# Scaled queries, a row minimum as the exponential's bias, and one broadcast product in the softmax of a decoder layer

## What is computed

```python
q = _mxfp4_matmul(x, wq_codes, wq_scales) + bq      # w = codes * scales repeated over 32 rows
k = _mxfp4_matmul(x, wk_codes, wk_scales) + bk
v = _mxfp4_matmul(x, wv_codes, wv_scales) + bv
scores = einsum('bqhd,bkhd->bhqk', q, k) / sqrt(128)
attn = softmax(scores, axis=-1)
out = einsum('bhqk,bkhd->bqhd', attn, v)
x = x + _mxfp4_matmul(out, wo_codes, wo_scales) + bo
```

## Time and profile before

| | us |
|---|---|
| median of 3 runs | 530.16 |
| lowest and highest run | 528.49, 530.91 |
| span of the profiled execution (first to last instruction) | 527.9 |
| busy PE / DVE / ACT / POOL | 489.7 / 405.2 / 283.8 / 191.0 |
| length of one attention group, second to seventh | 38.8 |

### The profile page before, as it was taken

The page is one execution under the profiler, slowest core; times in us unless marked ns, Lnnn a source line. Parts: engine busy times, 40 slices in busy tenths (PEclk is TensorE's granted clock), DMA queues, the critical chain, the costliest instruction groups (busy, mean ns, idle before and its releaser), DMA issues.

```text
span 527.9 us, 11484 instructions
## 1 busy us (share of the span) xinstructions
PE 489.7 (93%) x3222; PEld 431.4 (82%) x3222; DVE 405.2 (77%) x1040; ACT 283.8 (54%) x804; POOL 191.0 (36%) x232
## 2 busy tenths in 40 slices
PE   6899999999999999999999998979998999898985
PEld 6688899899898898898898898769875667776764
DVE  6689988988988988988988888787784753344465
ACT  2667656655655666666656564655425545522231
POOL 3417512312313313303303034426116666365640
PEclk9999999999999999999999999999989999999999
DMA  6441211210211211211100793299953456445544
GB/s 191 120 116 57 74 32 31 71 30 30 70 30 30 70 30 30 70 30 39 60 0 0 268 324 129 89 296 305 292 186 100 146 175 213 132 128 158 153 145 159
DMA packets 63269, 60.77 MB, mean 115 GB/s; under 512 B 5552, under 2 KB 60544, under 8 KB 63104
## 3 DMA queue, kind: packets, MB, share of 16 engines
q1 hardware_dynamic: 59024, 49.64, 31.0%
q0 software_dynamic: 3936, 10.55, 7.2%
q10 hardware_dynamic: 272, 0.13, 0.1%
HBM read 47.82 MB, written 20.87 MB: 130 GB/s over the span
## 4 chain that ended last, share of the span: by engine, by line
PE 63%; DVE 18%; issue 6%; ACT 6%; POOL 3%; DMA 1%; another core or an unknown queue 1%; DVEq 0%; SPq 0%; ACTq 0%; POOLq 0%
PE bank L998 12%; PE bank L1000 11%; PE bank L999 11%; PE bank L1239 11%; PE bank L1247 6%; DVE qk_lo L1759 4%; DVE rmax L1767 3%; DVE nmax L1771 3%; PE bank L1079 3%; ACT qk_hi L1497 2%; ACT prob L1505 2%; PE bank L1243 2%; DVE pT_lo L1792 1%; PE bank L1004 1%; PE bank L1373 1%
## 5 line engine op out<-in xcount | busy, mean ns | idle before, releaser
L1505 ACT ACTIVATE prob<-bank,nmax 128x256 f32<-128x256 f32 x128 | 59.5, 470 | 105.2 <-DVE nmax L1771 103.3
L711 POOL TENSOR_TENSOR w_lo<-st_c,w_hi 128x512 fp32r<-128x512 f32 x32 | 41.2, 1286 | 197.0 <-ACT w_hi L1468 197.0
L1239 PE MATMUL bank<-moe_w,xT 128*128 x252 | 66.0, 385 | 2.0 <-DVE xT L2067 1.8
L1759 DVE SCALAR_TENSOR_TENSOR qk_lo<-bank,b_col,qk_hi 128x512 fp32r<-128x512 f32 x64 | 47.8, 748 | 14.3 <-ACT qk_hi L1497 13.5
L998 PE MATMUL bank<-hT_hi,w_lo 128*128 128x512 f32 x128 | 52.7, 412 | 4.5 <-DVE qk_lo L1759 3.3
L1767 DVE TENSOR_REDUCE rmax<-bank 128x2 f32<-128x512 f32 x64 | 43.8, 685 | 13.8 <-PE bank L1000 13.3
L1239 PEld LDWEIGHTS bank<-moe_w,xT 128*128 128x128 f32 x252 | 45.2, 190 | 8.7 <-issue 2.9
L1000 PE MATMUL bank<-hT_hi,w_hi 128*128 128x512 f32 x128 | 50.6, 395 | 0.0
L999 PE MATMUL bank<-hT_lo,w_hi 128*128 128x512 f32 x128 | 50.5, 394 | 0.0
L1497 ACT ACTIVATE qk_hi<-bank,b_col 128x512 fp32r<-128x512 f32 x64 | 44.0, 687 | 8.6 <-PE bank L1000 7.2
L1785 DVE TENSOR_SCALAR prob<-prob,rinv 128x256 f32<-128x256 f32 x128 | 46.3, 403 | 2.3
(11 more groups left out here) (272 smaller groups left out, 1493.2 us busy)
## 6 DMA issues: line engine op xcount, KB each, us to landing
y_dram<-ysb SPq DMA_DIRECT2D x63, 128.0 KB
moe_w<-in_w_gate SPq DMA_DIRECT2D x8, 512.0 KB, 8.1
moe_w<-in_w_up SPq DMA_DIRECT2D x8, 512.0 KB, 7.8
moe_w<-in_w_down SPq DMA_DIRECT2D x4, 1024.0 KB, 9.0
st_c<-in_wq_codes SPq DMA_DIRECT2D x16, 128.0 KB
st_c<-in_wk_codes SPq DMA_DIRECT2D x16, 128.0 KB
st_c<-in_wv_codes SPq DMA_DIRECT2D x8, 256.0 KB
st_c<-in_wo_codes SPq DMA_DIRECT2D x8, 256.0 KB
```

Of the source, the lines that this page charges most:

```text
L1239: mm = pe.matmul(o, xT_of(kt), w, start=kt == 0, stop=kt == KT - 1)
L1505: ex = act.activation(prob[:, i % 4, qt, :], bS[i % 2][:, qt * S:(qt + 1) * S], ACT.Exp, bias=nmax[:, i % 2, qt:qt + 1], scale=SCALE, accu ...
L1759: dve.scalar_tensor_tensor(out=qk_lo[:, hp, m, n * HALF:(n + 1) * HALF], in0=src[:, :], scalar=b_col[:, bass.ds(g_h + m * H, 1)], in1=qk_h ...
```

## The change

The query weights' scales and the query bias are multiplied by minus the softmax scale, once for each chunk (POOL) and once for all (DVE). The scores in the bank are then the negated scaled ones, so their row minimum is the bias that the exponential needs, with -1 as its scale; `rmax`, `nmax`'s own instruction and the semaphore between them go. The normalisation of a pair becomes one product of 128x512 with the reciprocals broadcast over the keys. POOL's four numbers are loaded one by one.

```diff
@@ -288,7 +288,6 @@
         h_seg = pT_lo[:, :, :, :].rearrange("p a b k -> p a (b k)")
 
         yg = [nc.alloc_sbuf_tensor_at(f"yg{n}", [P, 2, NT, D], F32, offset=at) for n, at in enumerate(yg_at)]
-        rmax = sb("rmax", [P, 2, 2])
         nmax = sb("nmax", [P, 2, 2])
         rsum = sb("rsum", [P, 2, 2])
         rinv = sb("rinv", [P, 2, 2])
@@ -417,7 +416,7 @@
         a_copy, t_turn, t_tab = sem("a_copy"), sem("t_turn"), sem("t_tab")
         p_rows = sem("p_rows")
         p_many = sem("p_many")
-        p_wm = sem("p_wm")
+        p_wm, p_q = sem("p_wm"), sem("p_q")
         a_wh = sem("a_wh")
         p_wl = sem("p_wl")
         v_ln = sem("v_ln")
@@ -425,7 +424,7 @@
         t_ln, a_ln, v_lnlo = sem("t_ln"), sem("a_ln"), sem("v_lnlo")
         t_b, v_b = sem("t_b"), sem("v_b")
         t_sc = sem("t_sc")
-        v_m1, v_max = sem("v_m1"), sem("v_max")
+        v_max = sem("v_max")
         a_exp = sem("a_exp")
         v_ri, v_p = sem("v_ri"), sem("v_p")
         t_pT, a_pT, v_pT = sem("t_pT"), sem("a_pT"), sem("v_pT")
@@ -694,9 +693,19 @@
 
         @block.gpsimd
         def _(pool):
+            scaled = [0]
+
+            def scale_queries(c):
+
+                scaled[0] += 1
+                pool.tensor_scalar(st_s[c][:, 0, :], st_s[c][:, 0, :], -SCALE, None, ALU.mult).then_inc(p_q, 1)
+                pool.wait_ge(p_q, scaled[0])
+
             def prep(c, wm, load_count, into):
 
                 wait(pool, d_w[c], load_count)
+                if c in (H0, H1):
+                    scale_queries(c)
                 if c == WC:
                     codes_v, scale_v = st_c[c][:, :, :], st_s[c][:, :, :]
                 elif c == VC:
@@ -882,10 +891,9 @@
                 pool.indirect_dma_start(out=x_all[:, t, :], out_offset=None, in_=x2_dram,
                                         in_offset=bass.IndirectOffsetOnAxis(ap=dest[:, t:t + 1], axis=0)).then_inc(d_xt, 16)
 
-            at = [pool.alloc_register(f"need{k}") for k in range(TOPK)]
             pool.wait_ge(v_slot, S_NEED)
             apart(pool)
-            pool.reg_load(at, need[0:1, :])
+            needed = [pool.value_load(need[0:1, k:k + 1], min_val=1, max_val=TILES) for k in range(TOPK)]
             pool.wait_ge(d_xt, 16 * NT)
             own(pool.tensor_scalar(y_slot[:, :, :], ordered, -1.0, None, ALU.mult))
             for n, (t, k) in enumerate(gather_order):
@@ -894,7 +902,7 @@
                 if k == 3:
                     pool.wait_ge(v_sh, NT)
                 pool.wait_ge(t_gu, SH + min(USED, FIRST_BESIDE + n * 15 // 16))
-                pool.wait_ge(y_done, pool.snap(at[k], min_val=1, max_val=TILES))
+                pool.wait_ge(y_done, needed[k])
                 apart(pool)
                 pool.indirect_dma_start(out=home(k)[:, t, :], out_offset=None, in_=y_dram,
                                         in_offset=bass.IndirectOffsetOnAxis(ap=y_slot[:, t, k:k + 1], axis=0)).then_inc(d_yg[t][place_of(k)], 16)
@@ -1503,7 +1511,7 @@
                 wait(act, t_pT, p - 3 if not (pl.first and i < 4) else 0)
                 for qt in range(2):
                     ex = act.activation(prob[:, i % 4, qt, :], bS[i % 2][:, qt * S:(qt + 1) * S], ACT.Exp,
-                                        bias=nmax[:, i % 2, qt:qt + 1], scale=SCALE,
+                                        bias=nmax[:, i % 2, qt:qt + 1], scale=-1.0,
                                         accum_out=rsum[:, i % 2, qt:qt + 1])
                 ex.then_inc(a_exp, 1)
 
@@ -1729,7 +1737,8 @@
             statistics()
             variances()
             dve.wait_ge(t_b, 1)
-            dve.tensor_copy(b_col[:, :], bJ[0][:, 0:3 * H]).then_inc(v_b, 1)
+            dve.tensor_scalar(b_col[:, 0:H], bJ[0][:, 0:H], -SCALE, None, ALU.mult)
+            dve.tensor_copy(b_col[:, H:], bJ[0][:, H:3 * H]).then_inc(v_b, 1)
             ln_low(dve, 0, 0, FIRST[0])
             reciprocals()
             rows()
@@ -1764,11 +1773,8 @@
             def maxima(pl, i):
                 p = pl.pair(i)
                 wait(dve, t_sc, p + 1)
-                dve.tensor_reduce(rmax[:, i % 2, :], bS[i % 2][:, :].rearrange("p (q k) -> p q k", q=2),
-                                  AX.X, ALU.max).then_inc(v_m1, 1)
-                wait(dve, v_m1, p + 1)
-                wait(dve, a_exp, p - 1 if not (pl.first and i < 2) else 0)
-                dve.tensor_scalar(nmax[:, i % 2, :], rmax[:, i % 2, :], -SCALE, None, ALU.mult).then_inc(v_max, 1)
+                dve.tensor_reduce(nmax[:, i % 2, :], bS[i % 2][:, :].rearrange("p (q k) -> p q k", q=2),
+                                  AX.X, ALU.min).then_inc(v_max, 1)
 
             for pos, t in enumerate(PRO_TILES):
                 if pos == 2:
@@ -1781,10 +1787,8 @@
                 wait(dve, a_exp, pl.pair(j) + 1)
                 dve.reciprocal(rinv[:, j % 2, :], rsum[:, j % 2, :]).then_inc(v_ri, 1)
                 wait(dve, v_ri, pl.pair(j) + 1)
-                for qt in range(2):
-                    sc = dve.tensor_scalar(prob[:, j % 4, qt, :], prob[:, j % 4, qt, :],
-                                           rinv[:, j % 2, qt:qt + 1], None, ALU.mult)
-                sc.then_inc(v_p, 1)
+                dve.tensor_tensor(prob[:, j % 4, :, :], prob[:, j % 4, :, :],
+                                  rinv[:, j % 2, :].unsqueeze(2).to_broadcast([P, 2, S]), ALU.mult).then_inc(v_p, 1)
 
             def prob_low(pl, j):
```

## The result

The changed kernel took 516.8 us (median of 4 runs, 515.8 to 518.6) beside 529.4 us for the kernel before on the same chip (4 runs, 528.5 to 530.9): a ratio of 0.9745, with a 95% interval of 0.9711 to 0.9779. That is 12.5 us by the medians and 13.5 by the ratio (which is computed over the runs and isn't the quotient of these two medians, 0.976), where 10.1 were forecast. The profiled execution took 516.5 us, its span 514.7 us against 527.9 before: 13.2 us.

A forecast was written before the change was run, and what follows sets the result against it. PE was taken to bound the kernel nearly everywhere in attention, so only its stops counted. 7.6 + 1.1 - 0.4 + 1.0 + 0.8 = 10.1 us off the median of 530.16 gave 520.1 us, range 516.5 to 525.5.

The forecast's parts named there:

- the first part: Attention: PE bounds nearly everywhere; its waits for DVE's qk_lo lengthen three slots, 1.26 us in a repeat.
- Part 1, the crossings: Slots 6, 7 and the next group's 0: without nmax they fall to 4.69 us; 7.6 us for six, 1.1 for the first.
- Part 2, the product: Normalisation: one broadcast product takes 0.69 us, waits 0.6 for POOL in slot 7 (bounds nothing and 1.28); no loss.
- the room of 0.85 us: DVE per slot: 3.84 us of work against PE's 4.69, so 0.85 us of waiting costs nothing.
- Part 3, POOL's scaling: Chunk preparation: sixteen 128x128 instructions, 0.55 us each, 0.64 with the wait, hidden in the repeats.
- The start: Before attention: POOL's scaling shifts DVE's layer norm, 0.3 us lost, plus 0.1 for the bias column; 0.4 together.
- The first group: Attention's first two heads: PE's 0.91 us wait for v_lo at 47.70 shrinks; 1.0 us won, between 0 and 1.1.
- The last group: Attention's last two heads: PE's 0.88 us wait at 318.09 shrinks without nmax; 0.8 us won, between 0.3 and 1.1.
- part 5: Before POOL's wait for gathered rows: four single loads take 3.1 us instead of 0.78, hidden, costing nothing.
- A: Rival, chance 0.17: in slots 6, 7 and 0 the product waits a whole POOL instruction, losing half the crossings' gain; 524.5 us.
- B: Rival, chance 0.09: PE's stops stay because something equally late stands behind nmax; only the ends move, 528.8 us.
- C: Rival, chance 0.06: the product waits for POOL's whole train, up to 3.2 us, 1.5 lost per crossing; slower, 539.6 us.

The follow-up runs named there:

- kernel with the bias alone: The changed kernel with the two products by a scalar put back in the normalisation; 518.98 us, ratio 0.9769 against the kernel before.
- kernel with the product alone: The kernel before with the broadcast product and the four single loads; 531.74 us, ratio 1.000 against the kernel before.
- the longer train: The changed kernel with POOL's scaling of the query's scales done four times, the last three by 1; 520.76 us, ratio 0.9804 against the kernel before.

## Where the prediction was right, and where it was wrong

The mechanism of the crossings was right. The steps that failed are three terms of the sum outside the repeats: a loss of 0.4 us at the start, where the runs show none (the first transposes of attention came 0.8 earlier, 0.64 of it by chance); 1.0 for the first group, which measured 1.8; and 0.8 for the last, which measured 1.2.

**Which engine bounds, and what DVE's delay costs** (the first part) held. PE bound attention, only its stops were worth anything, and all those from 60 to 262 us went with nmax. One reading was incomplete: POOL works in slots 1 and 2 too, from 144.88 to 147.42 us before, and those slots are not longer. There nmax, begun at 146.07 when w_lo was nearly done, took 0.17.

**Part 1, the crossings.** 7.6 us were forecast for six crossings and 1.1 for the first; the starts of the transposes give 7.5 and 1.1. The slot fell to 4.69 and the repeat to 37.5, as forecast. The kernel with the bias alone shows that it is this part, and the kernel with the product alone that it is nothing else. What the working left out is that nmax's price belongs to its place beside POOL: with nmax kept and POOL's new work in place only 0.74 of 1.31 us are lost.

**Part 2, the product.** 0.69 us in quiet slots, as forecast from the row of the same shape. Beside POOL I had taken a wait of 0.6 in slot 7 between ends of nothing and 1.28; measured are 0.85, 0.48 and 0.38 in slots 6, 7 and 0. So the traces decide what the earlier trace rows left open: this instruction, with two inputs in the same memory, waits for POOL. The Trainium skill's rule ("SBUF — State Buffer", section "SBUF: two separate sides"), that a VectorE instruction with two inputs in SBUF and a GpSimd instruction that reads SBUF exclude each other for a whole instruction, is borne out beside POOL's 128x512 products and subtractions. Beside its 128x128 scaling it isn't borne out to the full length that the profile records, as the start shows below. The wait doesn't turn into time, as the room of 0.85 us takes it in.

**Part 3, POOL's scaling.** 0.53 to 0.56 us each, up to 0.85 behind a DVE product that got in, 0.55 forecast; hidden in the repeats, as forecast.

**The start.** I put a loss of 0.4 us; the first transposes of attention came 0.8 earlier, most of it by chance. I had reasoned that more work on POOL delays DVE's layer norm. It is the other way round. Before, one of DVE's small steps at 7.1 us meets POOL's first product and waits for it, 1.13 us. In the kernel with the product alone, whose start is that of the kernel before, the same wait meets the step behind, a product of two 128x4 tensors. DVE at the start of that kernel:

```profile
7.12 0.17 DVE L937 TENSOR_SCALAR nt<-nt 128x4 f32<-128x4 f32 x1
7.33 1.28 DVE L939 TENSOR_TENSOR rstd<-rstd,nt 128x4 f32<-128x4 f32 x1
8.64 2.33 DVE L947 TENSOR_SCALAR h_row<-x_in,mv,rstd 128x256 f32<-128x256 f32 x4
```

In the kernel after, POOL's short scaling stands there first, and the same steps are through before its long product. DVE at the start of the kernel after:

```profile
7.15 0.24 DVE L946 TENSOR_SCALAR nt<-nt 128x4 f32<-128x4 f32 x1
7.42 0.16 DVE L948 TENSOR_TENSOR rstd<-rstd,nt 128x4 f32<-128x4 f32 x1
7.62 2.23 DVE L956 TENSOR_SCALAR h_row<-x_in,mv,rstd 128x256 f32<-128x256 f32 x4
```

POOL in the same stretch, first of the kernel before, then of the kernel after:

```profile
6.97 1.27 POOL L708 TENSOR_TENSOR st_c<-st_c,st_s 128x512 f32<-128x512 f32 x1 [2.99 <-DMA st_s<-in_wk_scales]
```

```profile
6.80 0.56 POOL L701 TENSOR_SCALAR st_s<-st_s 128x128 f32<-128x128 f32 x1 [2.81 <-DMA st_s<-in_wk_scales]
7.44 1.28 POOL L717 TENSOR_TENSOR st_c<-st_c,st_s 128x512 f32<-128x512 f32 x1
```

So h_row begins about 1 us earlier: between 7.50 and 7.76 us in the seven kernels with the scaling, between 8.49 and 8.65 in the three without it. Beside the scaling itself the small steps hardly wait. DVE and then POOL in the kernel with the bias alone:

```profile
7.29 0.17 DVE L948 TENSOR_TENSOR rstd<-rstd,nt 128x4 f32<-128x4 f32 x1
```

```profile
7.14 0.56 POOL L701 TENSOR_SCALAR st_s<-st_s 128x128 f32<-128x128 f32 x1 [3.15 <-DMA st_s<-in_wk_scales]
```

Little of this reaches PE in the two executions that are compared. PE's first transposes begin at the later of two: the rows, and the end of PE's warm-up, whose 40 recorded matmuls took from 6.29 to 7.56 us in executions that differ in nothing there. The warm-up before and after:

```profile
4.03 7.20 PE L1004 MATMUL bank<-ident 128*128 128x128 f32 x40 [4.03 <-POOL ident L719]
```

```profile
4.04 6.56 PE L1012 MATMUL bank<-ident 128*128 128x128 f32 x40 [4.04 <-POOL ident L728]
```

In both it ended behind the rows: before, the rows are done at 10.83 us and the transposes begin at 11.07; after, at 9.85 and 10.43. The 0.64 us between the two starts are the difference of the warm-ups, so that much of the 0.8 is not the change's. Where the warm-up is short, the rows do count: the first projection began at 13.11 us with the scaling and a warm-up of 6.34, and at 14.18 without it and with 6.29, where PE waited 0.37 for h_row. Where it is long, nothing is left: 14.26 with the scaling (7.56), 14.27 without (7.48). Over six kernels with the scaling the mean is 13.6, over three without 14.2, a gain of some 0.5 us on average, of which the mean warm-ups (6.84 and 6.99) make up 0.15. A loss isn't seen in any. The earlier trace rows together could have told me: the step waits for an instruction of some 1.1 us and more, and the new one ahead of it is 0.55 long.

**The first group** was mis-sized: 1.0 us forecast, 1.8 measured. I counted the one stop that the earlier trace rows showed at 47.70, 0.91. The slots lose more than their waits say. Slot 4 went from 5.17 to 4.68 and slot 5 from 5.05 to 3.70. Before, DVE's normalisation there paid for both of its instructions. DVE in the first group of the kernel before:

```profile
38.77 0.96 DVE L1771 TENSOR_SCALAR nmax<-rmax 128x2 f32<-128x2 f32 x1
...
40.43 1.56 DVE L1785 TENSOR_SCALAR prob<-prob,rinv 128x256 f32<-128x256 f32 x2
...
45.48 1.57 DVE L1785 TENSOR_SCALAR prob<-prob,rinv 128x256 f32<-128x256 f32 x2
```

The broadcast product in the same places takes 0.84 and 0.87. By the kernel with the bias alone all but 0.26 us of the 1.8 comes without the product; those 0.26 are all that the product earns.

**The last group**: 0.8 us forecast, 1.2 measured, just over the upper bound of 1.1.

**Behind attention and part 5** nothing was forecast. The four loads are free, though their price was wrong: 3.1 us were put down, four times the one load, and they and the register steps between them are over 2.6 us after they begin. The 0.9 us by which this stretch was shorter are within what it varies by.

By terms: the crossings came out within 0.1 us. The start (1.2 better than forecast), the first group (0.8), the last (0.4) and the stretch behind attention (0.9, not counted for the change) make up, with rounding, the 3.1 us by which the span's gain was larger. Of these, 0.64 at the start and the 0.9 behind attention are what executions vary by; the rest is mis-sized terms. Of the 3.3 us between 520.1 and the measured 516.8, 0.8 are that the kernel before took 529.4 us there and not 530.2.

The result lies at the very edge of the stated range. By the median the measured time is 0.3 us inside the low end; by the ratio it would be 515.9, 0.6 outside. That end took in no loss at the start, 1.1 us in each of the first and the last group, 1 us more for small stops of the first, and a median 1.7 lower by chance. The start and the last group passed their bounds, the first group (1.8 of 2.1) didn't. Its own terms add up to 516.6 and not 516.5.

**Rivals.** A (a wait for a whole POOL instruction that eats the gain) is refuted in its price: waits of up to 0.85 exist at the crossings, and cost nothing there until DVE is given 0.94 us more to do. B is refuted by the ten waits that are gone. C is refuted by the longer train.

## What to carry over

An instruction of a few numbers on VectorE can cost as much as a large one when it meets GpSimd's instruction; look for groups whose mean is far above their shortest member, and fold such steps into a neighbour that reads PSUM. Before you price a swap on an engine, work out its room per slot against the engine that bounds: inside the room a longer instruction was free here, and past it the loss was larger than the work added, because the waits grew too. Where you add work to an engine that others collide with, ask not only how long it is but what it moves: a short instruction put ahead of a long one can let another engine through. And before you count a gain at the very start, compare what the two executions did there that the change doesn't touch.

## What the runs showed of the hardware beyond the forecast

- POOL pays too. Its instruction behind a DVE product that has got in between takes longer in the record: 1.75 us for 1.28 (128x512), 0.85 for 0.53 (128x128).
- The size of the DVE instruction doesn't matter for the wait: a product of two 128x4 tensors took 1.28 us beside POOL's product of 1.27, where it takes 0.16 alone. The reductions, qk_lo and pT_lo, which read a bank, kept 0.67 to 0.75 us beside POOL.
- How long DVE waits depends on POOL's instruction too: beside its 128x128 scaling at the start the steps of 128x4 took 0.16 to 0.32 us, beside its 128x512 product up to 1.28.
- PE's 40 recorded warm-up matmuls at the very start took between 6.29 and 7.56 us from one execution to the next, and 32 of them 6.34: single profiles don't tell a first projection apart below 1 us. They go at 6 or 7 in a us at first and at 11 or 12 later; the step up came between 7 and 8 us in two of the ten executions and at about 10 in two, while the profile's granted clock reads 1.00 throughout.
